# Elementwise work of an attention block moved from VectorE to ScalarE and GpSimd, with another periodic order

## The reference

```python
# 1. convolution block, per batch
xn   = (x - mean) / sqrt(var_unbiased + 1e-5) * ln_w + ln_b      # over the 128 channels
bcdt = grouped_conv3x3(einsum(xn, w_bcdt))                       # 64 channels
BC, dt = split(bcdt); AB = softmax(dt + A, over tokens) * BC
x1   = w_out @ ((x @ AB^T) @ BC) + x
# 2. attention on tokens t = x1^T, per batch
u = ln(t)                                                        # norm over 128 channels
q, k, v = lrelu(u Wq + bq), lrelu(u Wk + bk), lrelu(u Wv + bv)   # lrelu(z) = z if z >= 0 else 0.2 z
scores = q k^T / 8, set to -2^32 + 1 for keys whose u is all zero
o  = softmax(scores) v + u
t2 = t + gamma * (o - mean(o)) / sqrt(var(o) + 1e-8) + beta
# 3. mixture of 8 experts on all 32768 tokens, one expert per token, capacity 5120
u2 = ln(t2); logits = u2 gate_w + gate_b; expert = argmax, slot = running count per expert
y  = t2 + prob * (relu(u2 w1[e] + b1[e]) w2[e] + b2[e])          # if slot < capacity
```

## Time and profile before

| | |
|---|---|
| median of 3 runs | 2245.27 us (2244.58 to 2247.03) |
| span of the profiled execution | 2248.0 us |
| busy: PE, PE weight load, DVE | 2012.7 (90%), 1635.1 (73%), 1881.6 (84%) |
| busy: ACT, POOL | 1179.7 (52%), 1055.6 (47%) |
| token program, until its last scatter | about 1690 us |
| expert program | about 557 us |

### The profile page before, as it was taken

How to read it: one execution, slowest core, us unless ns; L and a number is a source line. 1 busy time by engine, 2 the same in 40 slices (tenths; PEclk the granted TensorE clock), 3 DMA queues, 4 the chain that set the end, 5 groups by cost and what they waited for, 6 DMA issues and landing times. The chain is left out here.

```text
span 2248.0 us, 42376 instructions
## 1 busy us (share of the span) xinstructions
PE 2012.7 (90%) x13855; PEld 1635.1 (73%) x13855; DVE 1881.6 (84%) x6075; ACT 1179.7 (52%) x2216; POOL 1055.6 (47%) x1276
## 2 busy tenths in 40 slices
PE   1699999999999999999999999999847999999996
PEld 1367777777777677777677777777636999899895
DVE  3368999988989888898889898888865999899895
ACT  0235545545545544544554554554526777677773
POOL 3012435554444554444554444555363665555554
PEclk9789999999999999999999999999978999999998
DMA  4911112212111211111221211221116778788774
GB/s 169 385 33 48 48 48 54 78 51 57 48 48 49 81 53 54 52 48 48 68 67 48 58 48 48 62 67 38 36 35 186 205 223 256 253 249 265 253 246 175
DMA packets 163516, 244.00 MB, mean 109 GB/s; under 512 B 31040, under 2 KB 110479, under 8 KB 163297
## 3 DMA queue, kind: packets, MB, share of 16 engines
q1 hardware_dynamic: 146016, 209.46, 30.7%
q0 software_dynamic: 17280, 31.84, 4.4%
HBM read 115.95 MB, written 95.56 MB: 94 GB/s over the span
## 5 line engine op out<-in xcount | busy, mean ns | idle before, releaser
L1080 PE MATMUL pvp<-va,pT 128*128 128x129 f32 x4096 | 492.1, 275 | 1.5 <-DVE rc L905 0.8
L1080 PEld LDWEIGHTS pvp<-va,pT 128*128 128x128 f32 x4096 | 479.7, 191 | 15.5 <-issue 6.7
L1251 POOL DMA_INDIRECT token_rows<-res x284 | 310.8, 1094 | 225.9 <-DVE res L1384 154.6
L730 DVE TENSOR_REDUCE mxs<-mxp 128x1 f32<-128x512 f32 x512 | 336.4, 683 | 16.3 <-PE mxp L957 12.7
L530 POOL DMA_INDIRECT expert_slots<-rows,slot_i x256 | 277.3, 1083 | 90.1 <-issue 90.1
L487 POOL TENSOR_TENSOR rstd<-var,neghalf 128x4 f32<-128x4 f32 x128 | 164.7, 1286 | 319.7 <-DVE negm L721 316.6
L1437 PEld LDWEIGHTS e_yp<-w2s,hid 128*128 128x128 f32 x2272 | 295.0, 192 | 20.4 <-ACT hid L1314 0.3
L1437 PE MATMUL e_yp<-w2s,hid 128*128 128x128 f32 x2272 | 300.5, 275 | 0.0
L1052 PE MATMUL stp<-qhl,klh 128*128 128x512 f32 x512 | 248.4, 485 | 54.7 <-ACT pT L616 51.6
L616 ACT ACTIVATE pT<-stp 128x512 f32<-128x512 f32 x512 | 278.8, 595 | 32.9 <-PE stp L1054 28.5
L1314 ACT ACTIVATE hid<-e_hp,b1c 128x512 f32<-128x512 f32 x284 | 195.2, 687 | 115.2 <-PE e_hp L1429 106.9
(11 more groups left out here) (242 smaller groups left out, 4083.7 us busy)
## 6 DMA issues: line engine op xcount, KB each, us to landing
w1p<-w_parts SPq DMA_DIRECT2D x71, 512.0 KB, 4.5
expert_slots<-fill SPq DMA_DIRECT2D x32, 660.0 KB, 11.5
e_rows<-expert_slots SPq DMA_DIRECT2D x71, 264.0 KB, 2.9
w2s<-in_w SPq DMA_DIRECT2D x71, 256.0 KB, 4.5
xs<-in_x SPq DMA_DIRECT2D x32, 512.0 KB, 3.7
token_rows<-rows SPq DMA_DIRECT2D x32, 512.0 KB, 4.0
f_rows<-token_rows SPq DMA_DIRECT2D x32, 512.0 KB, 6.5
out<-f_cols SPq DMA_DIRECT2D x32, 512.0 KB, 7.3
```

Source lines behind the costliest of these rows:

```text
L730: v.reduce_max(mxs[:, qt, n % 2:n % 2 + 1], mxp[n % 2][:], AX).then_inc(s["mx_read"], 1)
L1080: last = mm(pvp[qt % 2][:, 0:VA], pT[c][:, kt, n * P:(n + 1) * P], va[k][:, kt, :], start=(kt == 0), stop=(kt == NT - 1))
L1251: g.indirect_dma_start(out=tokens, out_offset=bass.IndirectOffsetOnAxis(ap=res[n % 2][:, q, TOKEN:TOKEN + 1].bitcast(I32), axis=0), in_=re ...
```

## The change

- The leaky ReLU of q and k: 0.2 z + relu(0.8 z). ACT now makes two passes over `work`, (L723 Identity, L724 Relu) and POOL adds them (L617). DVE's L724 of before goes.
- The product with gamma moves from DVE to POOL, as a step `ln2m` of its own (L620).
- All-zero keys are now those whose first-norm variance is zero: POOL, 128 x 8 (L609). DVE's maximum over u (L801) goes, and `mask` no longer needs `u1n`.
- Each norm's statistics are one step: 8 `bn_stats`, 8 `bn_aggr`, with tiles of their own per norm. Variance scaling and minus mean go to POOL (L593, L594), then power and product, all of them 128 x 8 instead of 128 x 4. The third norm's results are written into `rows` directly.
- `pos` is some instructions shorter (`eoff`, `rc`, `rd` go).
- The order is new: the loop runs over c = 5 to 24, with a batch of the convolution block three ahead of the oldest batch in attention, the routing steps one behind it, and the rest in longer `head` and `tail` lists.

```diff
-        steps = [("u1n", 3), ("mx", 1, 0), "x_turn", ("st", 0, 0), ("st", 0, 1), ("mx", 1, 1), ("st", 0, 2),
...
+        steps = [(("mx", 0, 3), 1), (("st", 1, 2), 0), ("h", 2), ("t1b", 0), (("st", 1, 3), 0), (("mx", 0, 4), 1),
...
-            for c in range(1, B - 2):
-                one_pass(one, c)
+            for c in range(5, 25):
+                for st, ahead in steps:
+                    one(st, *batch(c + ahead))
...
@@ gpsimd
-            def rsqrt(var, negm, rstd, shift, j, have, done, b):
-                own = slice(4 * j, 4 * j + 4)
-                wait_apart(pool, have, b * 8 + (4 * j + 4), passed["pool"])
-                g.tensor_tensor(rstd[:, own], var[:, own], neghalf[:, own], ALU.pow).then_inc(done, 1)
-                wait_apart(pool, done, b * 4 + (2 * j + 1), passed["pool"])
-                g.tensor_tensor(shift[:, own], negm[:, own], rstd[:, own], ALU.mult).then_inc(done, 1)
+            def rsqrt(mv_, var, negm, rstd, shift, have, done, b, eps, scale=1.0):
+                wait_apart(pool, have, b * 2 + 2, passed["pool"])
+                g.tensor_scalar(var, mv_[:, :, 1], scale, eps, ALU.mult, ALU.add).then_inc(done, 1)
+                g.tensor_scalar(negm, mv_[:, :, 0], -1.0, 0.0, ALU.mult, ALU.add).then_inc(done, 1)
+                wait_apart(pool, done, b * 4 + 1, passed["pool"])
+                g.tensor_tensor(rstd, var, neghalf[:], ALU.pow).then_inc(done, 1)
+                wait_apart(pool, done, b * 4 + 3, passed["pool"])
+                g.tensor_tensor(shift, negm, rstd, ALU.mult).then_inc(done, 1)
...
+                if st == "qk_lrelu":
+                    wait_apart(pool, s["qkz_ready"], b + 1, passed["pool"])
+                    g.tensor_tensor(qk[:], qk[:], qka[:], ALU.add).then_inc(s["qk_ready"], 1)
+                if st == "ln2m":
+                    wait_apart(pool, s["on_ready"], b + 1, passed["pool"])
+                    g.tensor_tensor(o[k][:], o[k][:], bc_mid(gamma_r[:], NT), ALU.mult).then_inc(s["ong_ready"], 1)
@@ scalar
-            def normalise(dst, src, rstd_, shift_, j, have, b, done):
-                if j % 2 == 0:
-                    act.wait_ge(have, b * 4 + (j + 2))
+                if j == 0:
+                    act.wait_ge(have, b * 4 + 4)
...
-                    a.activation(qkz[:], workf, ACT.Identity, bias=bqks_c[:], scale=qkscale[:]).then_inc(s["qkz_ready"], 1)
+                    a.activation(qka[:], workf, ACT.Identity, bias=bqks_c[:, 1:2], scale=qkscale[:, 1:2])
+                    a.activation(qk[:], workf, ACT.Relu, bias=bqks_c[:, 2:3], scale=qkscale[:, 2:3]).then_inc(s["qkz_ready"], 1)
@@ vector
-                v.tensor_scalar(var[:, own], mv_[:, own, 1], scale, eps, ALU.mult, ALU.add).then_inc(got, 1)
-                v.tensor_scalar(negm[:, own], mv_[:, own, 0], -1.0, None, ALU.mult).then_inc(got, 1)
...
-                if st == "qk_lrelu":
-                    lrelu(qk[:], qkz[:]).then_inc(s["qk_ready"], 1)
-                if st == "kflag":
-                    v.reduce_max(kabs[:], u1[k][:], AX, apply_absolute_value=True).then_inc(s["kabs_ready"], 1)
...
-                    v.tensor_tensor(o[k][:], o[k][:], bc_mid(gamma_r[:], NT), ALU.mult).then_inc(s["ong_ready"], 1)
```

More of the change, by code:

```diff
@@ L147, in token_program @@
         u1T = sb("u1T", [P, N])
-        kabs, kflag = sb("kabs", [P, NT]), sb("kflag", [P, NT])
+        kflag = [sb(f"kflag{k}", [P, NT]) for k in range(2)]
         kt = sb("kt", [NT, P], F32R)
@@ L236, in token_program @@
[L236 to L240, removed]
+        steps = [(("mx", 0, 3), 1), (("st", 1, 2), 0), ("h", 2), ("t1b", 0), (("st", 1, 3), 0), (("mx", 0, 4), 1),
[10 rows of a table added]
+                 (("mx", 1, 7), 1), (("pv", 0, 1), 1), ("bT_turn", 3), (("negmax", 1), 1), ("mask", 2),
[3 rows of a table added]
@@ L453, in _ @@
             chain(g.tensor_scalar(rank[:], iota_i[:], -1.0, float(E), ALU.mult, ALU.add))
-            chain(g.tensor_scalar(eoff[:], iota_i[:], float(CAP), 0.0, ALU.mult, ALU.add))
             chain(g.iota(tokid_i[:], pattern=[[1, NT]], base=0, channel_multiplier=NT))
@@ L472, in _ @@
             chain(g.memset(gwc[:], 0.0))
-            chain(g.memset(qkscale[0:U, :], 0.125))
-            chain(g.memset(qkscale[U:P, :], 1.0))
+            for i, part in enumerate((1.0, LEAK, 1.0 - LEAK)):
+                g.memset(qkscale[0:U, i:i + 1], 0.125 * part)
+                chain(g.memset(qkscale[U:P, i:i + 1], part))
             chain(g.memset(img[:], 0.0))
@@ L541, in _ @@
             act.wait_ge(s["mask_ready"], 1)
-            a.activation(bqks_c[:], bqk_c[:], ACT.Identity, scale=qkscale[:]).then_inc(s["const_act"], 1)
+            for i in range(3):
+                last = a.activation(bqks_c[:, i:i + 1], bqk_c[:], ACT.Identity, scale=qkscale[:, i:i + 1])
+            last.then_inc(s["const_act"], 1)
             act.wait_ge(s["const_act"], 1)
             def normalise(dst, src, rstd_, shift_, j, have, b, done):
-                if j % 2 == 0:
-                    act.wait_ge(have, b * 4 + (j + 2))
+                if j == 0:
+                    act.wait_ge(have, b * 4 + 4)
                 for t in range(2 * j, 2 * j + 2):
@@ L707, in _, with stats @@
                 w1_part(e)
-            def stats(src, bn_, mv_, var, negm, j, got, b, eps, scale=1.0):
-                own = slice(4 * j, 4 * j + 4)
-                for t in range(4 * j, 4 * j + 4):
+            def stats(src, bn_, mv_, got, used, b):
+                if b >= 1:
+                    wait_apart(dve, got, b * 2, passed["dve"])
+                for t in range(NT):
                     last = v.bn_stats(bn_[:, t, :], src[:, t, :])
                 last.then_inc(got, 1)
-                wait_apart(dve, got, b * 8 + (4 * j + 1), passed["dve"])
-                for t in range(4 * j, 4 * j + 4):
+                wait_apart(dve, got, b * 2 + 1, passed["dve"])
+                if b >= 1:
+                    dve.wait_ge(used, b * 4)
+                for t in range(NT):
                     last = v.bn_aggr(mv_[:, t, :], bn_[:, t, :])
                 last.then_inc(got, 1)
-                wait_apart(dve, got, b * 8 + (4 * j + 2), passed["dve"])
-                v.tensor_scalar(var[:, own], mv_[:, own, 1], scale, eps, ALU.mult, ALU.add).then_inc(got, 1)
-                v.tensor_scalar(negm[:, own], mv_[:, own, 0], -1.0, None, ALU.mult).then_inc(got, 1)
-            def lrelu(dst, zs):
-                return v.scalar_tensor_tensor(out=dst, in0=zs, scalar=0.2, in1=zs, op0=ALU.mult, op1=ALU.max)
             def mx_read(b, c, n):
@@ L855, in one @@
                     v.tensor_tensor(rows[k][:, :, 0:C], rows[k][:, :, 0:C], o[k][:], ALU.add).then_inc(s["t2_ready"], 1)
-                if what == "ln3s":
+                if st == "ln3s":
                     dve.wait_ge(s["t2_ready"], b + 1)
-                    stats(rows[k][:, :, 0:C], bn3, mv3, var3, negm3, j, s["t2_stats"], b, 1e-5)
+                    stats(rows[k][:, :, 0:C], bn4, mv4, s["t2_stats"], s["t2_rstd"], b)
                 if what == "negmax":
@@ L889, in one @@
                     v.tensor_copy(oh_bf[:], oh[:]).then_inc(s["ohb_ready"], 1)
+                    v.tensor_scalar(r8[:, 5, :], r8[:, 4, :], -float(CAP), float(E * CAP), ALU.mult, ALU.add)
                 if st == "pos":
```

152 lines of the change are left out of this document (69 added, 83 removed), and 221 rows, old and new, of tables (head, steps, tail).

## The result

The changed kernel takes 2239.43 us (median of 13 runs, 2236.43 to 2242.55) against 2245.27 for the kernel before (13 runs, 2241.66 to 2250.39). The prediction said 2219, a gain of 26 us; the gain is 5.8. The spans of the two profiled executions are 2240.1 and 2248.0 us, so the two traces have 7.9 us to explain, 2.1 more than the medians differ by.

What follows compares the result with a forecast made beforehand. PE bounds the token loop: 43.9 us of work plus 0.4, 0.35, 0.1, 0.3 and 2.0 make 47.0, rounded to 47.3 against 48.3. Thirty passes give -30, with start and end -26: 2245.3 becomes 2219 us, range 2153 to 2265.

Steps and rivals of the forecast that it cites:

- what the change frees: PE in the token loop: all 4.4 us lost per pass removed; 45.3 us if POOL's sum costs PE nothing (rival, 0.23).
- rival (c): ACT's place in the order still sets PE's waits for exponentials; 3.5 of 4.4 us stay, 2245 us; chance 0.10.
- The small stalls that were named: New PE waits per pass: transpose of u 0.4 us, `qk` 0.35, v 0.1.
- the meeting at v: POOL's sum of q and k holds a small DVE instruction in `pos`; PE waits 2.0 us per pass, bounds 0 to 2.4.
- rival (b): Gamma product also meets DVE at `va` behind v; DVE loses 0.6 to 1.6 us, pass 48.5 to 49.5, 2267 us; chance 0.22.
- The term "1.0 less, 30 times": Token loop: a pass of 47.3 us instead of 48.3, counted 30 times, gives -30 us.
- the start: First batches: +1 us as the norm's halves go; the new order could cost up to 10, or nothing.
- The end: Last batch, uncovered: gamma on POOL +1.1 us, second norm +1, third norm +1.
- the sign "some 76% of the token program": DVE's busy share in the changed profile, expected beside a pass of 47.3 us; DVE's work falls to 36 us.

Runs made afterwards that it cites:

- e1: Changed kernel, with POOL's sum of q and k also waiting until VectorE has written the slot numbers (`slot_i`): 2173.89 us, 0.9677 of the kernel before.
- e3: Changed kernel with two waits on POOL, the sum of q and k for `slot_i` and the gamma product for `va`: 2172.16 us, 0.9671 of the kernel before.
- e2: Changed kernel, with only POOL's gamma product also waiting until VectorE has written `va`: 2227.81 us, 0.9915 of the kernel before.

## Why the prediction was wrong, step by step

**Right: what the change frees.** Prediction: without a meeting PE reaches 45.3 us per pass. e1 and e3 run at 45.30, with PE busy throughout. That it fits to 0.1 us is partly luck: the loader's smaller waits, counted as some 20 us behind the earlier trace rows, are 36 us in the trace, by which the same sum has 5.2 us lost per pass and not 4.4. The waits of PE in the earlier trace rows were waits of order, and the new order removes them; rival (c) is refuted. The small stalls that were named are there as waits of the loader of 0.25 to 0.4 us each.

**Right: the meeting at v.** The sum starts 2.4 us after the `qk` matmuls end (717.58 to 720.00; forecast 2.5), holds one of L1008 to L1015 for over 1.5 us in 24 of 25 passes, and costs 1.82 us of each (e2 to e3; forecast 2.0). The one caught is in 22 of them L1010 and not `rb` (L1008), which is through when the sum begins.

**Wrong, and the cause of the miss: one meeting, not two.** The step that failed is "Against it: if DVE is on time, `va` is over before gamma starts", by which rival (b) was kept out of the sum. The forecast's own first meeting makes VectorE late, so in the case forecast the condition could not hold. The numbers stood there: `va` near 8.8 us after the `qk` matmuls, gamma from 7 to 9.4. In the trace `va` begins at 7.45 and gamma at 6.45. (With VectorE on time, in e1, `va` isn't over either when gamma starts: it is only first, and that is enough.) VectorE loses 1.17 us by it, inside the 0.6 to 1.6 of (b), and a pass 0.67. (b) had put most of VectorE's loss on PE and 0.6 more on a later logit chain, 1.6 in all; there is no such second part, so the time lies between the forecast and (b).

**The term "1.0 less, 30 times".** It was -30; the passes gave -15.1. With the second meeting taken away (e2) they give -31.2: its sums of `y` for batches 3 and 31 start at 221.2 and 1545.8, 1324.6 us apart, against 1355.8 before. So the whole miss of this term, 15 us, is the meeting left out, 0.67 x 24 = 16 us. Two smaller errors in it cancel: a pass before is 48.45 and not the 48.3 of the one interval in the earlier trace rows, which makes the gain of a pass 1.33 in e2; and only 24 passes have it, since those of 221 to 320 us lose 2.6.

**Wrong: the start, and the end.** The start was put at +1, "could cost up to 10"; it is +8.0, mis-sized by 7 us, and the trace points at PE's missing work at 100 to 160 us. The end was put at +3 and is -0.8: the second norm's ACT passes of the last batch begin at 1644.97, 83.0 us after the last `y`, against 86.7 in the earlier trace rows, so the drain's new order seems to give more than the longer chain takes; no run separates the two. (The last scatter ends 116.3 us behind the last `y` instead of 118.6; the expert program, whose code is the same, is 1.5 us longer in this trace.)

Together, of the profiled span: 14.9 us in the passes, 7.0 at the start, less 3.8 at the end, is the 18.1 by which 2240.1 stands above the forecast 2222.

**Mis-sized without effect.** VectorE gave up 6.0 us per pass, not 7.0 (from 43.15 to e1's 37.18, by the windows). With the holds it is busy 84% of a steady pass; of the token program as a whole it is 78%, so the sign "some 76% of the token program" came true in name, while the 36 us in a pass of 47.3 behind it did not. A power of 128x8 is 1.64 to 1.67 us, where 1.8 had been taken.
